# The first score products ahead of gelu's sums, and two row scores ahead of the first feed-forward product, on other PSUM banks

## The reference

```python
xn = layernorm(x)
q1, q2 = split(xn @ Wq.T)                    # 16 heads of 32, twice
s1, s2 = q1 @ k1.T, q2 @ k2.T                # 8 key heads, each for two query heads
w = softmax(s1) - lam * softmax(s2)
attn = w @ v                                 # per head
attn = attn * rsqrt(mean(attn**2) + 1e-5) * g * (1 - LAMBDA_INIT)
x = x + attn @ Wo.T
h = layernorm(x) * ln1_g + ln1_b
h = gelu(h @ ternary(w1).T + b1)             # 512 -> 2048
h = layernorm(h) * ln2_g + ln2_b
x = x + h @ ternary(w2).T + b2               # 2048 -> 512
```

## Time and profile before

| | us |
|---|---|
| time, median of 3 runs | 2291.74 (2291.2 to 2291.82) |
| the profiled execution, its own time | 2290.26 |
| its span, first to last instruction | 2288.5 |
| PE busy | 2139.8 (94%) |
| DVE busy | 1783.9 (78%) |
| ACT busy | 1516.7 (66%) |
| POOL busy | 1066.2 (47%) |
| mean granted TensorE clock | 0.962 |

### The profile page before, as it was taken

How to read it: one execution, slowest core, us unless ns; L and a number is a source line. 1 busy time by engine, 2 the same in 40 slices (tenths; PEclk the granted TensorE clock), 3 DMA queues, 4 the chain that set the end, 5 groups by cost and what they waited for, 6 DMA issues and landing times.

```text
span 2288.5 us, 45380 instructions
## 1 busy us (share of the span) xinstructions
PE 2139.8 (94%) x18239; PEld 1184.0 (52%) x18239; DVE 1783.9 (78%) x2700; ACT 1516.7 (66%) x1973; POOL 1066.2 (47%) x803
## 2 busy tenths in 40 slices
PE   7777999999999999999999999999999999999988
PEld 5444555554555555455555555555555555555443
DVE  3678878787987968788787878888786888878773
ACT  3467676766667676666767666676766667675754
POOL 2312726436272643627264363726436372643526
PEclk9869999999999999999999999999999999999999
DMA  7414122130423213031331303132150323212020
GB/s 291 125 46 95 44 80 70 34 97 23 117 48 84 65 35 101 22 98 48 87 78 40 103 16 97 48 93 56 44 118 13 98 46 94 56 46 68 2 57 19
DMA packets 253009, 160.16 MB, mean 70 GB/s; under 512 B 171812, under 2 KB 221580, under 8 KB 252288
## 3 DMA queue, kind: packets, MB, share of 16 engines
q1 hardware_dynamic: 249792, 152.07, 25.4%
q0 software_dynamic: 3008, 5.20, 0.8%
HBM read 51.82 MB, written 20.38 MB: 32 GB/s over the span
## 4 chain that ended last, share of the span: by engine, by line
PE 67%; DVE 16%; ACT 7%; issue 4%; POOL 3%; DMA 2%; SPq 0%; POOLq 0%; ACTq 0%; DVEq 0%
PE ps L1608 17%; PE ps L1626 11%; PE ps L1511 5%; PE ps L1636 5%; PE ps L1458 4%; PE ps L1543 4%; PE ps L1460 4%; PE ps L1459 4%; DVE attn_raw L1155 2%; PE ps L1572 2%; ACT arena L873 2%; PE ps L1573 2%; POOL attn_raw L687 2%; PE ps L1571 2%; DVE arena L1125 2%
## 5 line engine op out<-in xcount | busy, mean ns | idle before, releaser
L687 POOL TENSOR_TENSOR attn_raw<-attn_raw 128x512 f32<-128x512 f32 x448 | 629.4, 1424 | 48.1 <-ACT attn_raw L844 21.9
L1608 PE MATMUL ps<-rows,w1T 128*128 128x512 f16 x2048 | 483.9, 379 | 22.8 <-DVE rows L1246 22.8
L1125 DVE TENSOR_REDUCE arena<-ps 128x6 f32<-128x924 f32 (+1 forms) x330 | 349.3, 1083 | 41.5 <-PE ps L1511 40.9
L663 POOL TENSOR_TENSOR q<-q 128x512 f16<-128x512 f32 x128 | 190.5, 1492 | 333.5 <-ACT q L803 332.5
L1251 DVE SCALAR_TENSOR_TENSOR arena<-attn_raw,vec_cols,arena 128x512 f16<-128x512 f32 x256 | 299.3, 1173 | 34.2 <-ACT arena L842 34.1
L1626 PE MATMUL ps<-w2T,arena 128*128 128x512 f16 x1440 | 325.9, 379 | 0.0
L1608 PEld LDWEIGHTS ps<-rows,w1T 128*128 128x128 f16 x2048 | 193.3, 97 | 242.6 <-DVE rows L1246 35.2
L839 ACT ACTIVATE attn_raw<-ps,vec_cols,wstep 128x512 f32<-128x512 f32 x256 | 198.9, 777 | 180.0 <-PE ps L1608 177.3
L674 POOL TENSOR_TENSOR arena<-arena,out_const 128x512 f32<-128x512 f32 x64 | 102.0, 1605 | 458.1 <-DVE arena L1287 457.0
L1155 DVE TENSOR_TENSOR attn_raw<-arena,attn_raw 128x1024 f16<-128x1024 f32 (+1 forms) x128 | 193.7, 1544 | 84.9 <-ACT attn_raw L819 82.7
L1458 PE MATMUL ps<-arena,wqT_hi 128*128 128x512 f16 x512 | 208.2, 407 | 31.6 <-ACT arena L814 25.0
(11 more groups left out here) (192 smaller groups left out, 4410.4 us busy)
## 6 DMA issues: line engine op xcount, KB each, us to landing
stack_raw<-q SPq DMA_DIRECT2D x744, 64.0 KB, 2.0
arena<-in_x SPq DMA_DIRECT2D x64, 256.0 KB, 2.9
out<-arena SPq DMA_DIRECT2D x64, 256.0 KB, 2.0
arena<-in_x SPq DMA_DIRECT2D x14, 1024.0 KB, 5.5
arena<-in_L_ffn_w SPq DMA_DIRECT2D x7, 1024.0 KB, 13.8
rows<-in_x SPq DMA_DIRECT2D x2, 1024.0 KB, 6.8
stack_raw<-in_L_xattn_Wq SPq DMA_DIRECT2D x8, 256.0 KB, 9.6
k_att<-k_store SPq DMA_DIRECT2D x4, 495.0 KB
```

What stands on the lines that cost most here:

```text
L687: ins = pool.tensor_tensor(acc[:, e, :], acc[:, e, :], src[:, j % NG, :], ALU.add)
L1125: dve.tensor_reduce(negmax[:, tt:tt + 2, u0:u1], ps[:, bank:bank + 2, 0:(u1 - u0) * S].rearrange("p b (u s) -> p b u s", s=S), AX.X, ALU.m ...
L1608: ins = pe.matmul(ps[:, B_H + j % 2, :], w1T[:, k, j * P:(j + 1) * P], rows16[:, e, k, :], start=(k == 0 and e == 0), stop=(k == KD - 1 an ...
```

## The change

There are four edits. In `ATTEND`, `s0` goes ahead of `g` (PE alone does both letters), and `t2` ahead of `v6` (DVE alone has both in its stream with a new order). Row blocks go round the banks in the order 0, 1, 6, 7 and no longer 6, 7, 0, 1, and query 7 goes to bank 3. In the feed-forward loop of PE, for j = 0, the first two row blocks come ahead of `hidden(i, 0)`. ACT copies query 6 behind `h_hi` and no longer ahead of it. The waits follow the banks.

```diff
@@ ATTEND
-    "c e1 k14 k15 e2 g y0 y1 s0 l0 q0 s1 l1 q1 s2 v0 l2 h1 s3 v1 l3 h2 t0 y2 z0 z1 s4 v2 l4 q2 z2 s5 v3 l5 q3 t1 s6 v4 l6 h3 "
-    "s7 v5 l7 h4 v6 t2 y3 z3 v7").split()]
+    "c e1 k14 k15 e2 s0 g y0 y1 l0 q0 s1 l1 q1 s2 v0 l2 h1 s3 v1 l3 h2 t0 y2 z0 z1 s4 v2 l4 q2 z2 s5 v3 l5 q3 t1 s6 v4 l6 h3 "
+    "s7 v5 l7 h4 t2 v6 y3 z3 v7").split()]
@@ row_bank
-            return (B_O, B_L, 0, 1)[tb % row_banks(c)]
+            return (0, 1, B_O, B_L)[tb % 4] if c else (B_O, B_L)[tb % 2]
@@ query_bank
-            return (B_L, B_Q, B_Q, B_Q, B_L, 0, 1, 0)[n]
+            return (B_L, B_Q, B_Q, B_Q, B_L, 0, 1, 3)[n]
@@ iteration, ACT
-                    for n in range(QATT, QEARLY):
+                    for n in range(QATT, QEARLY - 1):
                         q_hi(i + 1, n)
                 h_hi(i)
                 if ahead:
-                    for n in range(QEARLY, QM):
+                    for n in range(QEARLY - 1, QM):
                         q_hi(i + 1, n)
@@ output_vectors, PE
                     pe.wait_ge(s_l2, 2)
+                    wait(pe, s_q32, 1, QM, QM)
@@ queries, PE
                 elif n == 7:
-                    wait(pe, s_q32, c, QM, 6)
+                    wait(pe, s_mid, c - 1, TT, TT)
@@ row_scores, PE
                     wait(pe, s_tmax, c, NT, tb - row_banks(c) + (2 - tb % 2 if c else 1))
+                elif tb == 0 and c:
+                    wait(pe, s_q32, c, QM, QM - 1)
                 elif tb == 2:
-                    wait(pe, s_q32, c, QM, QM)
+                    wait(pe, s_ht_lo, c - 1, KD, KD)
@@ ffn_late, PE
                         wait(pe, s_gg_lo, c, JH, j + 1)
+                        if j == 0 and c + 1 < NBLK:
+                            wait(pe, s_q32, c + 1, QM, QM)
@@ iteration, PE
                 for j in range(JH):
                     beside = maxima_beside(j) if ahead else []
-                    hidden(i, j)
+                    if j:
+                        hidden(i, j)
                     if i == 0:
                         output_vectors(j)
                     for tb in beside[:2]:
                         row_scores(i + 1, tb)
+                    if j == 0:
+                        hidden(i, j)
                     if j >= FLAG:
```

## The result

The changed kernel takes 2255.9 us in the median of 4 runs (2252.3 to 2258.6), against 2291.8 us before: a ratio of 0.984, with a 95% interval of 0.983 to 0.986. It is 36 us faster, 16 us short of the forecast of 2240 and inside its range. The profiled execution took 2255.11 us (span 2253.3, clock 0.976), so 35.2 us less than the profiled one of before.

What follows compares the result with a forecast made beforehand. The prediction took PE, busy for 94% of the span, as the bound, leaving only its idle time and clock; 46.2 + 5.4 = 51.6 us off the median of 2291.74 gave 2240 us, range 2232 to 2266.

Steps and rivals of the forecast that it cites:

- Moving `s0`: Start of attention: `s0` ahead of `g` fills query 0's wait of 1.79 us; `s2` comes 3.4 us earlier per block.
- The slack of the maxima: Ahead of `s0`: the stored maxima land 0.2 to 0.8 us before `s0` needs them at its earlier start.
- the first edit's sum: `s0` ahead of `g`: 14 blocks gain 3.4 us each, block 15 loses up to 1.3 us; -46.2 us in all.
- The clock: Query 0 behind the one-column sums: the fall to half clock goes, since no idle time is left beside them.
- the partial rival: The fall goes in some blocks only (2 us per fall), or POOL holds the feed-forward part (5.4 us); 2245 to 2262 us; chance 0.18.
- The rival with a fall in every block: Query 0 still runs at half clock behind the sums; 1.4 us gained per block, 2268 us; chance 0.12.
- The row scores: Feed-forward start: two row blocks ahead of `hidden(0)`, query 6's copy behind `h_hi`; 5.4 us gained, between nothing and 11.4.
- So the gain is cut to 0.36 us per block: Row block 6 still waits for DVE's maximum, so 0.36 of 0.76 us per block remains; 15 blocks give 5.4 us.
- `t2` ahead of `v6`: DVE in attention: one tile reaches its transposing DMA some 0.9 us earlier; counted as nothing, at most 15 us.
- The slower rival: Feed-forward start: the clock falls to half around PE's idling and transposes; 2315 us; chance 0.04.

Runs made afterwards that it cites:

- attend_only: The kernel before with the new `ATTEND` alone (`s0` ahead of `g`, `t2` ahead of `v6`); 2246.7 us, ratio 0.980.
- no_power: Changed kernel with POOL's power left out of the chain that `y0` and `y1` wait for; 2244.6 us, ratio 0.979.
- pool_later: Changed kernel with one wait more: POOL's first sum waits for DVE's low half of slice 1; 2247.5 us, ratio 0.981.
- short_sums: Changed kernel with POOL adding only 8 of 512 columns in its sums of slices 2 to 15; 2257.2 us in one execution.
- v6_first: Changed kernel with `v6` ahead of `t2` on DVE again; 2255.5 us, ratio 0.984.
- attend_and_maxima: Kernel before with the new `ATTEND`, and DVE taking both pairs of j = 0 maxima ahead of slice 0's low half; 2250.4 us, ratio 0.981.
- hidden_first_old_maxima: Changed kernel with PE's old order at j = 0 alone (`hidden(0)` ahead of row blocks 0 to 3); 2231.2 us, ratio 0.973.
- hidden_first_pool_later: hidden_first plus a wait holding POOL's first sum until DVE's low half of slice 1 is made; 2222.9 us, ratio 0.970.
- hidden_first: Changed kernel with PE's old order at j = 0, and DVE taking both pairs of j = 0 maxima ahead of slice 0's low half; 2222.0 us, ratio 0.970.

## Why the prediction was right, and where it was short

- **Moving `s0`: right, place and price.** The slack of the maxima held, query 0 lost its wait, DVE's `y1` became the next to be late, and `s1` and `s2` came within 0.1 us of the times worked out. attend_only shows that this edit alone gives 46 us (2292.5 on that chip less 2246.7; 44.0 between the profiled executions), as the first edit's sum said. In the changed kernel's profiled execution it gave 41.6 us: 1.4 us went to the four falls of the clock, and most of the rest to blocks 1 to 3, which had less to gain (`s2` at 13.0, 13.9 and 14.1 us behind the slot and not 14.3).
- **The clock: mostly right.** It stays up in 10 of 14 blocks, so "some blocks", the partial rival, is what happened. Its price of 2 us a block was too high: 0.35 us, since the wait for `y1` hides the rest. no_power shows the same fall at 1.4 us once that wait is gone. The rival with a fall in every block has a slip in its sum: 825.3, 1.66 and 2.60 make 829.6 and not 829.9, so 1.8 us gained per block and some 2263 us, not 2268.
- **The row scores: the step that failed.** The wait ahead of row block 0, the start of `hidden(0)` and the wait ahead of row block 6 came as worked out. The step "So the gain is cut to 0.36 us per block" ended there and took all behind it to follow at a fixed distance. It does not: POOL's first sum came 0.4 us sooner against the low half of slice 1, which was 0.37 us ahead of it and is now 0.03 us behind, and took 1.78 us for 0.75. Row block 10 pays for it. In place of +5.4 us the edit gave -5.6 in the profiled execution, 11.0 of the 16 us that are missing, and below the "nothing" that was its lower bound. pool_later and short_sums show the cause, from both sides.
- **The range held in part by luck.** The rival whose range the 2256 us fall in, 2245 to 2262, was to lose them by falls of the clock, which cost 1.4 us, or by POOL's sums as the limit of the feed-forward part. What cost most was in neither.
- **`t2` ahead of `v6`: right at nothing** (v6_first). Its bound of 15 us was far too wide.
- **The slower rival** (a fall of the clock at the feed-forward start) did not happen: its window around the transposes, 736 to 752 us in the changed kernel, has a clock of 1.00. So over 16 transposes with products right ahead of them and a short wait behind, the rule of the Trainium skill ("TensorE: Matmul & The Clock Gate", Part 4: PE-mode transpose) made no difference here. The last block is the exception, before and after alike: PE idles 4.84 us ahead of its transposes, and in the changed kernel the clock falls 0.3 us after their start. In attend_and_maxima, hidden_first_old_maxima and hidden_first_pool_later it falls 1.8 to 1.9 us ahead of them, in the idle time, so this fall does not need the transposes. The rows are PE's in the last block, then the windows around an inner block's transposes and of the last block's fall:

```profile
2181.33 3.38 PE L1601 MATMUL ps<-ident,attn_raw 128*128 128x128 f32 x16 [4.84 <-DVE attn_raw L1240]
```

```profile
736.00:752.00 16.00, 15.13 (x79) 7.68 (x77) 14.33 (x41) 8.75 (x17) 6.60 (x6) 1.00 0.13 33
2181.60:2185.00 3.40, 3.11 (x16) 2.70 (x14) 1.04 (x3) 0.26 (x1) 2.21 (x3) 0.50 0.00 0
```

- **What the change left:** its two halves are not alike. The attention edit is worth 46 us. Of the row-score edit the copy behind `h_hi` is worth having (28 us, with the banks), the two row blocks ahead of `hidden(0)` are not. With PE's old order there and DVE's maxima first, the kernel takes 2222 us, 34 us less than the changed one.

## What to carry to other kernels

When a stall is taken away, look for the next wait that it covered: here the slow query covered the wait for `y1`, and a later fall of the clock was in turn covered by that wait. Work put ahead of a waiting instruction helps only if its own inputs are there sooner; two row blocks ahead of a product that waited for `h_lo` brought the wait for a copy. And before an edit is taken to shift all behind it by a fixed amount, look in the trace for an instruction whose duration varies: where two engines' instructions start within a few tenths of a microsecond of each other, a small shift may turn their order and cost a whole microsecond. Here 0.08 us ahead was free for DVE, and 0.03 us behind cost it 1.04 us.

## What the runs showed of the hardware

DVE's `scalar_tensor_tensor` with two SBUF tensors of 128x512 takes 0.75 us alone and up to 1.9 us beside a POOL `tensor_tensor` of the same size; with that POOL work cut to 8 columns it takes 0.75 us in every slice that is left so and meets no full sum. The one that starts first is not hindered: DVE took 0.74 us when 0.37 or 0.08 us ahead of POOL, and 1.78 us when 0.03 us behind it. The second one pays, on either side: POOL's first addition (its spans are rough) took 1.26 us where DVE had finished (pool_later), 1.50 us with DVE 0.37 us ahead, and 1.79 us with DVE 0.08 us ahead. The Trainium skill states such a lock ("SBUF — State Buffer", "SBUF: two separate sides", on the port pair that VectorE and GpSimd share, held for a whole instruction), and these traces agree with it in kind. In size they come somewhat under it: DVE's 1.04 us more compare with 1.24 us that were left of POOL's addition.

The kernel before had blocks of nearly equal length, 133.0 us, with a fall of the clock in each at the same place. Once the idle time was filled, the falls came in some blocks only, and how many differed from one profiled execution to the next: none of 14 in attend_only, four in the changed kernel, seven in pool_later; and two in hidden_first but none in hidden_first_pool_later, whose steady blocks are equal. Around the last block's transposes the clock was at half in every kernel's profiled execution, for 3.4 us in some (the changed kernel, attend_only, hidden_first) and 13.7 us in others (attend_and_maxima, hidden_first_pool_later); from these transposes to the end of the span it took 71.9 to 72.0 us in the first and 75.1 us in the others. What decides between them is not shown. The medians of these kernels hold a few microseconds of such falls, so that steps of 1 us per block could be read from the steady blocks of a trace and not from the total time.
